# A two-layer transformer block on one core: expert rows added to their tokens in DRAM instead of stored by slot and gathered

## The chip, the core and the metric

The kernel runs on one core of one Trainium2 chip. The metric is the device time of one execution in microseconds; the time before is the median of three runs. The engines are PE (TensorE, matrix products), DVE (VectorE), ACT (ScalarE), POOL (GpSimd) and SP (SyncE, which here only issues transfers).

## What is computed

2048 tokens of 512 channels go through two adaLN layers. Layer 0 has windowed attention and a mixture of experts, layer 1 sliding-window attention and a Hadamard-mixed feed-forward part. The part that matters, cut down:

```python
probs = softmax(x @ gate_weight.T)                      # 64 experts
top_val, top_idx = lax.top_k(probs, 8)
top_val = top_val / top_val.sum(-1, keepdims=True)      # routing weight
# the last four choices of a token are sent to the most similar "primary"
# expert where that one is similar enough
rerouted = mapping[top_idx]; rerouted[:, :4] = top_idx[:, :4]
gate, up = split(expert_gate_up(x))                     # 192 + 192 wide
y = expert_down(silu(gate) * up)                        # 512 wide
out = zeros.at[tok].add(y * w)                          # sum over a token's 8 rows
x = x + gate_mlp * out                                  # adaLN residual, before layer 1
```

Everything is float32. A token's eight rows lie in up to eight expert tiles.

## The kernel before, in words

The program is a sequence of six stages with a barrier of all engines after each. Within a stage every engine has its own written-out list of turns, and semaphores join them; the function `schedule` of each stage says which tile each part of a turn works on. Nothing is planned at run time but the number of expert tiles in use.

1. **Setup** (0 to 32 us): constants, the modulation vectors of layer 0.
2. **First attention** (32 to 319 us), 16 tiles of 128 tokens. Its turn ends with the router: for each pair of tiles `choose` (L659 to L691) takes the eight best experts, writes a one-hot `route_hot` (token, choice, expert) in bfloat16 and the weights `route_w`. SP also fills the expert output `y_moe` in DRAM past its first 64 tiles (L418, L419: 32 transfers of 1 MB) and stores the normalized tokens `h_moe` (L424).
3. **Routing** (319 to 383 us). The rows of all experts are laid out in slots of tiles of 128, each expert rounded up to whole tiles, at most 192 tiles (`SLOTS`), here 158. PE counts and ranks (L899 to L932), DVE works out where each expert's tiles begin, and L943 to L949 build `slot_rows`, the token of each slot, as products of one-hot matrices paced by ACT and DVE. `map_row` (L940, L1041) holds where each expert was moved.
4. **Experts** (383 to 1212 us), one turn for each slot tile `g`. `turn(before, g, after)` has `before = g - 1` and `after = g + 1`. PE transposes the hidden rows of `before` (L1157), multiplies tile `g` by the gate and up weights (L1166), transposes the input rows of `after` (L1175) and multiplies `before` by the down weights (L1183). POOL gathers the 128 token rows of `after` by an indirect transfer (L1136 to L1146), after PE has transposed the tile two before. DVE makes the hidden rows (L1282) and scales the output rows into `y` (L1287). ACT stores `y` (L1214) into `y_moe` at its slot. SP loads 1.15 MB of weights for each of 64 experts into a ring of four. The loop is unrolled by two; iterations beyond the tiles in use are skipped by a test on each engine. In the first 15 double turns DVE also runs `place` (where each token's eight rows lie: `pos_u`) and `finish_mod`, in the next 15 a transform of the feed-forward weights.
5. **Second attention** (1212 to 1748 us), 16 tiles. Before a tile's statistics POOL gathers its eight expert rows from `y_moe` (L1440 to L1447; eight indirect transfers of 256 KB a tile, spread over the turn) and DVE adds them into `x_res` with their weights (L1719 to L1723, eight additions). Then come the statistics (L1725 to L1734), the reciprocal root on POOL (L1457), the normalization that opens the next turn on DVE (L1742), modulation on POOL (L1459, L1461), and PE's transposes (L1578) and products (L1599 for q, L1608 for k and v). In a turn, g is the tile gathered, y the tile added, p the tile projected, f, s, a and w the later steps.
6. **Feed-forward** (1748 us to the end), PE near its peak in float32r.

The lines around which the change turns:

```python
                        nc.gpsimd.indirect_dma_start(out=xg[:, b], out_offset=None, in_=h_moe,
                                                     in_offset=bass.IndirectOffsetOnAxis(ap=st_tok[:, b], axis=0)).then_inc(x_in[b], 16)
...
                        act.dma_start(dst, y[:, b]).then_inc(y_stored[b], 16)
```

## Time and profile before

| | |
|---|---|
| median of 3 runs | 2322.02 us (2320.09 to 2323.6) |
| the profiled execution's own time | 2322.45 us |
| its span, first to last instruction | 2320.6 us |
| PE busy | 2024.3 us (87%) |
| DVE busy | 1095.3 us (47%) |
| ACT busy | 742.9 us (32%) |
| POOL busy | 725.6 us (31%) |
| transfers, mean rate | 302.32 MB, 130 GB/s |
| DMA_INDIRECT L1145 (expert inputs) | 160, mean 990 ns of POOL |
| DMA_INDIRECT L1446 (expert outputs) | 128, mean 966 ns of POOL |

A busy time is the time in which an instruction of the engine ran. Where a row says `[1.54 <-PE bank L1183]`, the engine stood idle for 1.54 us before that instruction and was released by PE's line 1183. Issuing an indirect transfer is work of POOL; "to landing" is from the start of the issue to the arrival of the data. PEclk is the granted clock as a share of the full one. The times of the stages above are read from where their first instructions start.

### The profile page before, as it was taken

Reading aid. Unit: us, or ns where it says so; the run is one execution under the profiler, and the core shown is the slowest. Engines: PE = TensorE matmul, PEld = TensorE weight load, DVE = VectorE, ACT = ScalarE, POOL = GpSimd, SP = SyncE. Lnnn points to the kernel's source line nnn. Section 1 sums busy time; section 2 is a strip of 40 time slices with the busy share of each in tenths; the row PEclk is TensorE's granted clock in tenths of the full one; section 3 lists DMA queues with packets and bytes.
Section 4 is the critical chain, followed back from the end, with each engine's and each line's share of the span. In section 5 each row is a group of like instructions: output and inputs, shape, how many; then the busy total and the mean of one; then the engine's idle time right before and its main releaser. Section 6 shows DMA issues by size and latency. Waiting matters only on the chain. (4 is left out here: it accounts for less than half of the span.)

```text
span 2320.6 us, 38481 instructions
## 1 busy us (share of the span) xinstructions
PE 2024.3 (87%) x11149; PEld 1332.4 (57%) x11150; DVE 1095.3 (47%) x2952; ACT 742.9 (32%) x1743; POOL 725.6 (31%) x1163
## 2 busy tenths in 40 slices
PE   4799867999999999999971588888866999999998
PEld 2667534555555555555531255555545878878787
DVE  2467667555553222222114577777634444443432
ACT  0233226222222222222210255555642333222322
POOL 0243311222333333333226677777402101011000
PEclk7799879999999999999985689999987999999999
DMA  6556632565555656656625222223011112121210
GB/s 239 177 211 219 235 116 65 182 214 180 190 182 196 193 191 211 215 195 199 213 94 147 82 82 76 83 79 85 5 43 40 64 55 82 64 81 63 73 64 28
DMA packets 122554, 302.32 MB, mean 130 GB/s; under 512 B 24912, under 2 KB 28624, under 8 KB 122320
## 3 DMA queue, kind: packets, MB, share of 16 engines
q1 hardware_dynamic: 73424, 179.04, 22.7%
q0 software_dynamic: 23040, 75.52, 11.4%
q10 hardware_dynamic: 25984, 46.38, 5.3%
q8 instruction: 63, 1.03, 0.2%
q14 instruction: 43, 0.35, 0.0%
HBM read 216.47 MB, written 83.36 MB: 129 GB/s over the span
## 5 line engine op out<-in xcount | busy, mean ns | idle before, releaser
L1166 PE MATMUL bank<-arena 128*128 x1272 | 445.5, 493 | 10.3 <-issue 9.2
L1166 PEld LDWEIGHTS bank<-arena 128*128 128x128 f32 x1272 | 229.6, 190 | 147.7 <-issue 16.9
L1183 PE MATMUL bank<-arena 96*128 x632 | 297.5, 593 | 0.0
L1287 DVE TENSOR_TENSOR arena<-bank,mod 128x512 f32<-128x512 f32 x158 | 109.3, 692 | 214.8 <-PE bank L1183 214.8
L1904 PE MATMUL bank<-x_hi,w_hi 128*128 128x512 f32 x512 | 200.8, 392 | 6.0 <-DVE x_lo L2037 6.0
L1904 PE MATMUL bank<-x_hi,w_lo 128*128 128x512 f32 x512 | 199.4, 389 | 0.0
L1904 PE MATMUL bank<-x_lo,w_hi 128*128 128x512 f32 x512 | 199.2, 389 | 0.0
L1282 DVE TENSOR_TENSOR arena<-arena,bank 128x192 f32<-128x192 f32 x159 | 56.3, 354 | 301.0 <-ACT arena L1204 300.6
L1199 ACT COPY arena<-bank 96x256 f32<-96x256 f32 x158 | 58.2, 368 | 423.8 <-issue 221.7
L1145 POOL DMA_INDIRECT arena<-h_moe,arena x160 | 158.4, 990 | 75.1 <-issue 74.2
L1144 POOL TENSOR_TENSOR arena<-neg_half 128x1 f32<-128x1 f32 x160 | 31.3, 196 | 461.9 <-PE bank L1175 461.7
L2117 DVE SCALAR_TENSOR_TENSOR ffn_arena<-bank,ffn_arena,mod 128x512 f32<-128x512 f32 x64 | 48.1, 751 | 221.5 <-PE bank L1904 174.7
L1183 PEld LDWEIGHTS bank<-arena 96*128 96x128 f32 x632 | 107.3, 190 | 76.2 <-issue 76.2
L1494 ACT ACTIVATE arena<-arena 128x256 f32<-128x256 f32 x256 | 127.0, 500 | 44.9 <-DVE arena L1701 44.6
L1446 POOL DMA_INDIRECT route_hot<-y_moe,pos_u x128 | 123.7, 966 | 32.1 <-issue 27.7
L1723 DVE SCALAR_TENSOR_TENSOR x_res<-route_hot,route_w,x_res 128x512 f32<-128x512 f32 x128 | 112.8, 881 | 26.6 <-DMA route_hot<-y_moe,pos_u 18.0
L1578 PE MATMUL bank<-ident,down_scale 128*128 128x128 f32 x64 | 14.6, 369 | 124.0 <-POOL down_scale L1461 124.0
L1885 POOL TENSOR_TENSOR ffn_arena<-ffn_arena,neg_half 128x1 f32<-128x1 f32 x16 | 8.8, 548 | 362.0 <-DVE ffn_arena L2051 362.0
L1175 PEld LDWEIGHTS bank<-ident,arena 128*128 128x128 f32 x640 | 80.2, 141 | 58.8 <-issue 28.8
L1904 PEld LDWEIGHTS bank<-x_hi,w_hi 128*128 128x128 f32 x512 | 96.1, 188 | 28.7 <-issue 4.8
L1904 PEld LDWEIGHTS bank<-x_hi,w_lo 128*128 128x128 f32 x512 | 96.1, 188 | 20.3
L1904 PEld LDWEIGHTS bank<-x_lo,w_hi 128*128 128x128 f32 x512 | 96.2, 188 | 19.5
(326 smaller groups left out, 3738.6 us busy)
## 6 DMA issues: line engine op xcount, KB each, us to landing
arena<-in_moe_up SPq DMA_DIRECT2D x64, 768.0 KB, 5.0
y_moe<-arena ACTq DMA_DIRECT2D x158, 256.0 KB, 3.1
y_moe<-mod SPq DMA_DIRECT2D x32, 1024.0 KB
ffn_arena<-in_ffn_up SPq DMA_DIRECT2D x64, 512.0 KB, 3.2
arena<-in_moe_down SPq DMA_DIRECT2D x64, 384.0 KB, 5.8
arena<-in_L_wmod SPq DMA_DIRECT2D x12, 1024.0 KB, 11.3
x_res<-in_L_attn_x SPq DMA_DIRECT2D x1, 4096.0 KB, 18.5
h_moe<-arena SPq DMA_DIRECT2D x16, 256.0 KB, 6.8
```

Of the source, the lines that this page charges most:

```text
L1145: nc.gpsimd.indirect_dma_start(out=xg[:, b], out_offset=None, in_=h_moe, in_offset=bass.IndirectOffsetOnAxis(ap=st_tok[:, b], axis=0)).the ...
L1166: mm = nc.tensor.matmul(psum[2 + b][:, 0:2 * FI], xgT[:, b, k], up_ring[:, bass.ds((e % RING) * UPW + k * 2 * FI, 2 * FI)], start=(k == 0) ...
L1175: mm = nc.tensor.transpose(psum[b][:, k * P:(k + 1) * P], xg[:, b, k * P:(k + 1) * P], ident[:])
L1183: mm = nc.tensor.matmul(psum[6 + b][:], hiddenT[:, b, n], down_ring[:, bass.ds((e % RING) * DOWNW + n * C, C)], start=(n == 0), stop=(n == 1))
L1199: nc.scalar.copy(hiddenT[:, b], psum[4 + b][0:FH, 0:2 * P].rearrange("p (n q) -> p n q", n=2)).then_inc(hT_out, 1)
L1282: nc.vector.tensor_tensor(hidden[:, b], gate_act[:, b], psum[2 + b][:, FI:2 * FI], ALU.mult).then_inc(hidden_done, 1)
L1287: nc.vector.tensor_tensor(y[:, b], psum[6 + b][:], mod[:, 0, 5], ALU.mult).then_inc(y_out, 1)
L1446: nc.gpsimd.indirect_dma_start(out=yg[:, j], out_offset=None, in_=y_moe, in_offset=bass.IndirectOffsetOnAxis(ap=pos_u[:, t, j:j + 1], axis ...
L1494: nc.scalar.activation(some, some, ACT.Exp, bias=nmx[:, t % 2, n:n + 1], scale=-1.0, accum_out=esum[:, t % 2, n:n + 1]).then_inc(exp_done, 1)
L1723: nc.vector.scalar_tensor_tensor(x_res[:, t], yg[:, j], route_w[:, t, j:j + 1], x_res[:, t], ALU.mult, ALU.add).then_inc(y_sum, 1)
L1904: mm = nc.tensor.matmul(bank, x, y, start=(n == 0), stop=(n == len(passes) - 1))
L2117: nc.vector.scalar_tensor_tensor(inner, up_bank[:], scales[:, 1, f:f + 1], gate_act[:, b], ALU.mult, ALU.mult).then_inc(inner_done, 1)
```

## The change

`y_moe`, its fills and its gathers go. Two arrays `x_sum[0]` and `x_sum[1]` in DRAM take the token rows: in the first attention SP stores the residual `x_res` into the first and zeros into the second. In the expert stage tile t's output rows are added to `x_sum[t % 2]` by an indirect transfer that POOL issues with an add (`compute_op=ALU.add`), one row per slot, to the row of its token; unused slots go to 128 spare rows. It waits for the y of that tile and is issued one turn late, behind the gather. Before y's buffer is written again, the add of the tile two before must have landed. The routing weight is multiplied into the hidden rows on DVE: the weight of a token for each expert is made in the first attention and in the routing stage (eight more transposes and 16 more products on PE, four more copies on ACT) and stored behind the token's row in `h_moe`, so that the gather brings 576 numbers instead of 512. DVE reads the expert of the tile into a register and copies the column. `place`, `map_row`, `pos_u`, `route_hot` and `route_w` go. In the second attention SP loads a tile from both arrays two turns ahead, DVE adds the two once, and the statistics and the reciprocal root move forward in the turn.

```diff
-        h_moe = dram("h_moe", [S, C])
-        y_moe = dram("y_moe", [SLOTS * P, C])
+        h_moe = dram("h_moe", [S + P, C + E])
+        x_sum = [dram(f"x_sum{b}", [S + P, C]) for b in range(2)]
...
@@ first attention, choose(pair) @@
-                    st.did(nc.vector.tensor_tensor(route_w[:, 2 * pair:2 * pair + 2], top[:], over(l2[:, 4], TOPK), ALU.mult))
+                    st.did(nc.vector.tensor_tensor(two, two, over(l2[:, 4], E), ALU.mult))
+                    st.settle()
+                    for half, dense in enumerate((routed.first, routed.second)):
+                        st.did(nc.vector.tensor_tensor(dense[:, pair].rearrange("p (t e) -> p t e", e=E), two, routed.multi[:, pair, half], ALU.mult))
...
@@ first attention, SP @@
-                        for g in (E + 2 * s * FILL, E + (2 * s + 1) * FILL):
-                            sp.dma_start(y_moe[g * P:(g + FILL) * P].rearrange("(g p) c -> p g c", p=P), some).then_inc(filled, 16)
+                        sp.dma_start(x_sum[1][s * P:(s + 1) * P], zero[:, 0:C]).then_inc(filled, 16)
...
+                        sp.dma_start(x_sum[0][z * P:(z + 1) * P], x_res[:, z]).then_inc(x_kept, 16)
...
@@ routing: SP, ACT, PE, DVE @@
+                sp.wait_ge(w_out, 2)
+                sp.dma_start(h_moe[0:S, C:].rearrange("(t p) e -> p t e", p=P), routed.second.rearrange("p i (t e) -> p (i t) e", e=E)).then_inc(w_stored, 16)
...
+                for n in range(2):
+                    act.wait_ge(wT_mm, n + 1)
+                    nc.scalar.copy(routed.secondT[:, 4 * n:4 * n + 4].rearrange("p i n -> p (i n)"), psum[2 + n][:]).then_inc(wT_out, 1)
...
+                pe.wait_ge(moves_wide, 1)
+                for n in range(2):
+                    for i in range(4):
+                        at = psum[6 + n][:, i * P:(i + 1) * P]
+                        nc.tensor.matmul(at, routed.secondT[:, 4 * n + i], moves_f, start=True, stop=False)
+                        mm = nc.tensor.matmul(at, ident[:], routed.first[:, 4 * n + i], start=False, stop=True)
+                    mm.then_inc(w_mm, 1)
...
-                st.did(nc.vector.tensor_copy(slot_rows[:, 0:SLOTS], psum[1][:, 0:SLOTS]))
+                step(ts(empty, psum[1][:, 0:SLOTS], 0.0, pad_row, ALU.is_equal, ALU.mult))
+                st.did(nc.vector.scalar_tensor_tensor(slot_rows[:, 0:SLOTS], psum[1][:, 0:SLOTS], -1.0, empty, ALU.add, ALU.add))
...
@@ experts, POOL @@
+                def add_rows(t, b):
+
+                    wait_tile(pool, y_out, 1, t)
+                    st.did(nc.gpsimd.tensor_copy(st_dst[:, b], column(t)))
+                    st.settle()
+                    st.did(nc.gpsimd.tensor_tensor(spare, neg_half[:], neg_half[:], ALU.add))
+                    nc.gpsimd.indirect_dma_start(out=x_sum[b], out_offset=bass.IndirectOffsetOnAxis(ap=st_dst[:, b], axis=0), in_=y[:, b],
+                                                 in_offset=None, compute_op=ALU.add).then_inc(y_added[b], 16)
...
                     if after is not None:
                         t, b, half = after
                         wait_tile(pool, x_in[b], 16, shift(half, -1))
+                        wait_tile(pool, w_read, 1, shift(t, -2))
...
+                    if before is not None:
+                        t, b, half = before
+                        if not isinstance(t, int) or t:
+                            add_rows(shift(t, -1), 1 - b)
+                used = schedule(pool, turn, st, POOL_M)
+                pairs = (used + 1) // 2
+                st.base, st.k = pairs * POOL_M + (st.first - 2 * POOL_M), 0
+                add_rows(pairs * 2 + -1, 1)
+                for b in range(2):
+                    pool.wait_ge(y_added[b], pairs * 16)
...
@@ experts, ACT: the store of y goes @@
-                        act.dma_start(dst, y[:, b]).then_inc(y_stored[b], 16)
...
@@ experts, DVE @@
-                        nc.vector.tensor_tensor(hidden[:, b], gate_act[:, b], psum[2 + b][:, FI:2 * FI], ALU.mult).then_inc(hidden_done, 1)
+                        wait_tile(dve, w_read, 1, t)
+                        nc.vector.scalar_tensor_tensor(hidden[:, b], gate_act[:, b], row_w[:, b:b + 1], psum[2 + b][:, FI:2 * FI],
+                                                       ALU.mult, ALU.mult).then_inc(hidden_done, 1)
...
-                        wait_tile(dve, y_stored[b], 16, shift(half, -1))
+                        wait_tile(dve, y_added[b], 16, shift(half, -1))
                         nc.vector.tensor_tensor(y[:, b], psum[6 + b][:], mod[:, 0, 5], ALU.mult).then_inc(y_out, 1)
+                    if after is not None:
+                        t, b, half = after
+                        e = dve.value_load(tile_expert[0:1, bass.ds(t, 1)], min_val=0, max_val=E - 1)
+                        wait_tile(dve, x_in[b], 16, half)
+                        wait_tile(dve, hidden_done, 1, shift(t, -2))
+                        nc.vector.tensor_copy(row_w[:, b:b + 1], xg[:, b, bass.ds(e + C, 1)]).then_inc(w_read, 1)
...
@@ second attention, SP @@
+                def rows_in(t):
+
+                    if t >= XB:
+                        sp.wait_ge(x_sums, t - XB + 1)
+                    sp.dma_start(x_res[:, t], x_sum[0][t * P:(t + 1) * P]).then_inc(x_in[t % XB], 16)
+                    sp.dma_start(xb[:, t % XB], x_sum[1][t * P:(t + 1) * P]).then_inc(x_in[t % XB], 16)
...
@@ second attention, POOL: gather() and its calls go; the reciprocal root moves to the turn's end @@
-                gather(0, range(0, TOPK))
...
+                    if y is not None:
+                        pool.wait_ge(stats, y + 1)
+                        if y:
+                            pool.wait_ge(xhat, y)
+                        nc.gpsimd.tensor_tensor(r1[:, 1:2], st1[:, 7:8], neg_half[:], ALU.pow).then_inc(rstd, 1)
...
@@ second attention, DVE: eight add_expert() a tile go @@
+                def join_rows(t):
+                    dve.wait_ge(x_in[t % XB], 32 * (t // XB + 1))
+                    nc.vector.tensor_tensor(x_res[:, t], x_res[:, t], xb[:, t % XB], ALU.add).then_inc(x_sums, 1)
...
                     if a is not None:
                         sums(a)
+                    if y is not None:
+                        join_rows(y)
...
+                    if y is not None:
+                        statistics(y)
                     if s is not None:
                         maxima(s, 2)
```

## Rows read from the trace of the kernel before

**Rows 1.** Two stages (start:end): us, busy PE, PEld, DVE, ACT, POOL; clock, DMA, GB/s
```profile
383.00:1212.00 829.00, 800.94 (x2860) 451.20 (x2860) 289.67 (x749) 204.62 (x477) 252.33 (x640) 0.99 0.57 187
1212.00:1748.00 536.00, 379.03 (x2530) 231.83 (x2530) 343.86 (x975) 246.32 (x753) 323.42 (x375) 0.84 0.26 77
```

**Rows 2.** timeline of one expert tile: start us, us, engine line op
```profile
903.27 0.60 PE L1175 MATMUL bank<-ident,arena 128*128 128x128 f32 x4
...
903.71 1.88 PE L1183 MATMUL bank<-arena 96*128 x4
...
904.04 0.19 POOL L1144 TENSOR_TENSOR arena<-neg_half 128x1 f32<-128x1 f32 x1 [2.93 <-PE bank L1175]
...
904.69 0.99 POOL L1145 DMA_INDIRECT arena<-h_moe,arena  x1 [0.47 <-issue]
...
905.68 0.20 POOL L1139 COPY arena<-slot_rows 128x1 int32 x1
905.73 0.69 DVE L1287 TENSOR_TENSOR arena<-bank,mod 128x512 f32<-128x512 f32 x1 [1.54 <-PE bank L1183]
...
905.96 0.19 POOL L1141 TENSOR_TENSOR arena<-neg_half 128x1 f32<-128x1 f32 x1
...
908.24 0.60 PE L1175 MATMUL bank<-ident,arena 128*128 128x128 f32 x4
```

**Rows 3.** instructions of line L1157, whole run
```profile
L1157 PE MATMUL bank<-ident,arena x316: 270/274/314, 397.9 to 1197.0; 128*96 128x128 f32 x158
```

**Rows 4.** timeline of VectorE in the second attention: heads of turns
```profile
1267.68 0.55 DVE L1742 TENSOR_SCALAR down_scale<-x_res,arena 128x512 f32<-128x512 f32 x1 [7.46 <-POOL arena L1457]
...
1298.02 0.55 DVE L1742 TENSOR_SCALAR down_scale<-x_res,arena 128x512 f32<-128x512 f32 x1 [7.44 <-POOL arena L1457]
...
1624.19 0.55 DVE L1742 TENSOR_SCALAR down_scale<-x_res,arena 128x512 f32<-128x512 f32 x1 [1.64 <-POOL arena L1457]
...
1649.15 0.54 DVE L1742 TENSOR_SCALAR down_scale<-x_res,arena 128x512 f32<-128x512 f32 x1
...
1673.25 0.69 DVE L1748 TENSOR_TENSOR mod<-bank,mod 128x512 f32<-128x512 f32 x1 [3.25 <-PE bank L1653]
```

**Rows 5.** busy time in stretches of the second attention (columns as in rows 1)
```profile
1212.00:1240.00 28.00, 0.00 (x0) 0.00 (x0) 7.13 (x15) 0.00 (x0) 16.96 (x21) 0.50 0.88 255
...
1457.00:1511.00 54.00, 45.70 (x318) 28.51 (x314) 41.01 (x117) 30.74 (x94) 39.05 (x46) 0.91 0.28 81
```

**Rows 6.** timeline: single instructions of first attention and routing
```profile
123.40 3.73 PE L554 MATMUL bank<-arena 128*128 128x128 f32 x32
...
232.41 0.35 DVE L749 TENSOR_SCALAR arena<-bank,arena 128x128 f32<-128x128 f32 x1 [2.31 <-PE bank L563]
...
319.78 1.07 ACT L841 CAST arena<-bank 128x512 bf16<-128x512 f32 x2 [8.21 <-PE bank L906]
```

**Rows 7.** instructions of line L1161: PE's register load
```profile
L1161 PEldq TENSOR_LOAD <-tile_expert x159: 296/303/841, 390.5 to 1195.8; - x159
```

**Rows 8.** instructions of line L1145: whole run, then landing within 900 to 950 us
```profile
L1145 POOL DMA_INDIRECT arena<-h_moe,arena x160: 986/986/1353, 386.2 to 1191.1; - x160
...
DMA to landing us min/median/max: 3.3/3.8/4.4
```

**Rows 9.** timeline of VectorE: end of the expert stage
```profile
1212.01 0.10 DVE L1313 MEMSET arena<- 128x1 f32 x2 [9.23 <-issue]
```

**Rows 10.** timeline of PE: first q product of the second attention
```profile
1246.59 5.06 PE L1599 MATMUL bank<-arena,mod 128*128 128x512 f32 x8 [0.77 <-ACT mod L1514]
```

**Rows 11.** DMA queues within 900 to 1000 us: packets, MB, share of 16 engines
```profile
q1 hardware_dynamic: 2304, 10.62, 31.7%
q0 software_dynamic: 1600, 5.24, 18.3%
q10 hardware_dynamic: 2880, 5.24, 14.1%
```

More of the change, by code:

```diff
@@ L907, in _ @@
                     mm.then_inc(secT_mm, 1)
+                for n in range(2):
+                    for i in range(4):
+                        mm = nc.tensor.transpose(psum[2 + n][:, i * P:(i + 1) * P], routed.second[:, 4 * n + i], ident[:])
+                    mm.then_inc(wT_mm, 1)
                 for f in range(HAD0):
@@ L1372, in schedule @@
                 tile = lambda t: t if 0 <= t < NT else None
[L1373 to L1374 removed]
+                for m in range(-3, NT + 2):
+                    turn(y=tile(m + 3), p=tile(m + 2), f=tile(m + 1), s=tile(m), a=tile(m - 1), w=tile(m - 2))
             def slot(t, c):
@@ L1787, in turn @@
                         nc.vector.tensor_tensor(x_res[:, w], ba[:], x_res[:, w], ALU.add).then_inc(x_out, 1)
-                    if y is not None:
-                        for j in range(5, TOPK):
-                            add_expert(y, j)
-                    if y is not None:
-                        statistics(y)
                     if s is not None:
```

179 lines of the change are left out of this document (74 added, 105 removed).

## The prediction

> **What bounds the kernel now.** I read three views in this order: the busy time by stage, the timeline of a tile or turn inside a stage, and the durations of single instructions. The chain of waits ends in the last stage (the feed-forward of layer 1), which the change leaves alone, so it says nothing here. The stage table [rows 1] shows the two stages that matter: the experts take 829.0 us with PE busy 800.9, the attention after them 536.0 us with PE busy only 379.0. The expert stage is PE's, the second attention is a chain across engines.
>
> Inside an expert tile [rows 2] PE goes from one product to the next without a gap; the transposes L1175 recur after 908.24 - 903.27 = 4.97 us. POOL has slack: it waits for the transposes, starts its gather at 904.69, and idles again. Over the stage the 158 pairs of L1157 run from 397.9 to 1197.0 [rows 3], so a tile takes 799.1 / 157 = 5.09 us on average; the 0.12 above 4.97 (19 us in all) falls mostly into the part where VectorE also does side work. In the attention, L1742 opens a turn of VectorE [rows 4]. From tile 2 (1298.02) to tile 14 (1624.19) there are 12 turns of 27.18 us. Two of them hold 45.70 us of PE work, the first 28 us of the stage none at all [rows 5].
>
> **The change part by part.**
>
> *First attention.* The choosing of experts for a pair of tiles gets three 128-wide products and a settle for one 16-wide product. The 128-wide L749 takes 0.35 us [rows 6], overlapped a little less: +0.8 us on VectorE. Seven of eight times it is covered, as VectorE then waits 2.31 us for PE before L749. The last is exposed: +0.8. SP's 32 fills of 1 MB become 19 of 256 KB or little more and 16 stores of 256 KB; nothing waited for the fills, so 0.
>
> *Routing.* ACT gets two copies ahead of the work PE waits for; two such took 1.07 us (L841) [rows 6]. PE gets 16 products of 128x128 in float32; 32 took 3.73 us (L554), so 1.9, and a release, 0.2. The table's end becomes two dependent operations instead of one, +0.4. The table's own 40 us are paced by ACT and only shift. SP's store of the weights stands ahead of three weight loads; they shift too. Sum +3.6.
>
> *Expert stage, what goes.* The plain stores leave ACT's queue, and 16 placings leave VectorE. VectorE waits for PE before L1287 [rows 2], so this gives at most the 19 us above.
>
> *Expert stage, what comes.* VectorE reads a register and copies one column per tile; PE's register load takes 0.30 us [rows 7], so with its arithmetic and the copy 0.7 us, done before POOL needs it (below). The decisive part is POOL's order. In turn g it gathers tile g+1 and then adds tile g-2, whose rows are ready only one turn later. So the gather of k+4 stands behind the add of k; PE's turn k+3 transposes k+4 before it multiplies out k+2. This closes a loop from y(k) ready to y(k+2) ready. Its length from [rows 2]: release 0.1; index copy to addition 0.28, to transfer 0.65: 0.93; the add's issue *a*; two small operations and the same lead for the gather, 0.28 + 0.28 + 0.65 = 1.21; the landing *L* from the gather's start; release 0.1; transposes to y ready, 906.42 - 903.27 = 3.15. Together 5.49 + a + L, for two tiles. The issue of a gather lasts 0.99, at most 1.35 us; its landing is 3.8 in the median and 4.4 at most in 50 us of this stage [rows 8]. Accumulating transfers are not in this trace. Nearest is the gather itself, so I take values just above its own: a = 1.10, L = 4.0 (its rows also grow from 2048 to 2304 bytes). The loop is 10.59, a tile 5.30 us: 157 x 5.30 = 832.1 against 799.1, **+33.0**. Bounds: with 0.99 and 3.8 a tile takes 5.14 (+8); with 1.35 and 4.4 it takes 5.62 (+83). Below nothing: if the loop is shorter than 9.94, PE keeps its 4.97, -19. VectorE's column is ready about 0.9 after y(k), POOL asks for it about 2.1 after: covered. If that cover is gone, half of the excess is added per tile. The reuse of the y buffer leaves the add 2 x 4.97 - 0.69 (L1287) - 1.0 (its lead) = 8.2 us to land, against 3.8 for a gather: covered.
>
> *End of the expert stage.* VectorE's last 9.23 us are empty passes of the loop [rows 9]. POOL makes the same passes and then adds the last tile. It starts them when the add of the tile before is issued, some 3.1 us before VectorE starts its own (5.3 for the tile, less 0.1 + 0.93 + 1.10), so it is through at 6.1 where VectorE was at 9.2. Then come 0.93 and the add's landing: 4.0 gives +1.8, twice that +5.8. I take +3.5, nearer to the gather's.
>
> *Start of the second attention.* The first q product starts at 1246.59 [rows 10]. Before it come eight gathers one after another. Without them it waits for the weights. The first 28 us move 255 GB/s [rows 5], 7.1 MB, of which 16 gathers are 4.2 MB; three tiles of the new loads are 1.6 MB. 4.5 MB at that rate are 17.6 us, so with the spread of the issues 1232.5: -14.1. Tiles 1 and 2 then wait 7.46 and 7.44 us for the reciprocal root on POOL, which stands behind gathers [rows 4]; that goes: -14.9. Sum **-29.0**.
>
> *Turns.* The turn that starts at 1624.19 has the adds but no gathers: 24.96 us. The next has neither: L1748, about 0.5 after the head of a turn, comes at 1673.25, so 1672.75 - 1649.15 = 23.6 [rows 4]. The new turn keeps a 0.7 us join and the statistics, which mostly fall into waits for PE. I take 23.8: 12 x (27.18 - 23.8) + 1.2 = **-41.8**. What is late next is PE: its 22.9 us of work a turn [rows 5].
>
> **Sum.** 0.8 + 3.6 + 33.0 + 3.5 - 29.0 - 41.8 = -29.9 against the profiled execution, 2322.45 (span 2320.6 and 1.85 around it): 2292.5. That execution is 0.4 above the median of the three runs, 2322.02, so I say 2292.
>
> **A rule against the change.** The 20 gathers in 100 us occupy queue 0 for 18.3% of 16 engines, 0.92 us each; with the stores and the weights the engines are 64% busy [rows 11]. No row shows an add. The Trainium skill, "Collectives: The Full Stack", section "The bandwidth ceiling: the fold count and why AG ≠ RS ≠ AR", says that a reducing transfer sends two source reads down one read ring and so halves the rate. By that rule the add would occupy the engines about twice as long as a copy; the first rival below gives that time.
>
> **The rivals.** *Slower: the gather is late behind the add.* Place: the software queue in the expert stage. Price: each us more in a + L costs 157 / 2 = 78.5 us; from 0.38 us above my value (29.9 / 78.5) the change loses. If an add occupies the queue 0.92 us longer than a gather and the next gather meets all of that, L is 3.8 + 0.92 = 4.7, and with a = 1.35 the loop is 11.54: 5.77 a tile, +107 instead of +33: **2366**. For it: the engines are busy in bursts already, and the loop has no slack. Against: the gather starts 2.3 us after the add, which may be gone by then. *Faster: the loop stays hidden.* PE keeps 4.97, -19 instead of +33: **2240**. Against: that needs a + L of 4.45, below the median gather of 4.8. *Turns shrink less.* If join and statistics land on the path, turns stay at 24.96, 15 us less gain: **2307**. Against: VectorE is idle for 3.25 us before L1748 at the end of the turn from 1649.15 [rows 4], so it has room.
>
> **How the numbers follow.** Forecast 0.42, late gather 0.36, hidden loop 0.12, longer turns 0.10. The forecast's own range is 2267 to 2342, from the bounds of a and L. The range for 8 in 10, 2257 to 2390, leaves out most of the hidden loop and a late gather beyond 5.92 us a tile. A change under 0.2% (4.6 us) is about what this measurement can't tell from none. Faster by more than that: 0.36 of the forecast, the hidden loop 0.12, 0.07 of the longer turns, 0.55. Within: 0.03 + 0.03 + 0.02 = 0.08. Slower: 0.03 of the forecast and 0.34 of the late gather, 0.37.
>
> **What would show it.** Right: L1157 pairs every 5.3 us, each L1175 released by the gather, with POOL starting it some 2.2 us after the add; L1742 every 23.8 us; the first q product 19 us after the stage's start. Wrong: an issue of the add well over 1.1 us, landings of the gather over 4.5, VectorE's register read or the free y buffer in the loop instead; or PE without waits at 4.97.

## The result, and the profile after

The changed kernel takes 2445.21 us (median of 4 runs, 2431.36 to 2450.8) against 2321.06 (4 runs beside it): ratio 1.0525, 95% interval 1.0479 to 1.0571. It is slower, and the forecast of 2292 us, its range (to 2390) and its likeliest sign were wrong. The profiled execution took 2443.06 us, its span 120.7 us more than the one of before. Where only one execution of an experiment's kernel was timed, the text compares it with this profiled one.

The page of the changed kernel: span, PE's share, the clock in 40 slices, and four of the costliest groups (busy us, mean ns, idle time ahead and what ended it).

```profile
span 2441.3 us, 39558 instructions
...
PE 2092.7 (86%) x11188; PEld 1332.8 (55%) x11189; DVE 990.6 (41%) x2920; ACT 742.0 (30%) x1747; POOL 896.2 (37%) x1464
...
PEclk7899888999999999999999967999997999999999
...
L1219 PE MATMUL bank<-arena 128*128 x1272 | 460.3, 506 | 22.2 <-issue 18.7
...
L1174 POOL DMA_INDIRECT x_sum<-arena x158 | 251.3, 1590 | 52.4 <-issue 51.9
L1325 DVE TENSOR_TENSOR arena<-bank,mod 128x512 f32<-128x512 f32 x158 | 109.4, 692 | 378.7 <-PE bank L1236 378.7
...
L1228 PE MATMUL bank<-ident,arena 128*128 128x128 f32 x640 | 100.7, 280 | 82.1 <-DMA arena<-h_moe,arena 81.8
```

L1228, the transposes of a gathered tile, waited 81.8 us on the matmul side and 122.3 us on the weight-load side for the gather's DMA; L1175 of [rows 2], its counterpart, ran without a gap. VectorE's L1325 idles 378.7 us for PE. The add (L1174) holds POOL 1590 ns each time. The hidden transposes, the counterpart of L1157 in [rows 3], show the pace:

```profile
L1210 PE MATMUL bank<-ident,arena x316: 270/274/421, 406.0 to 1405.5; 128*96 128x128 f32 x158
```

From 406.0 to 1405.5 are 999.5 us for 157 tiles, **6.37 us a tile** against 5.09. The busy time in four stretches (columns as in [rows 1]): the expert stage, its even middle, the second attention, and nine of its turns:

```profile
400.00:1411.00 1011.00, 887.17 (x2856) 461.99 (x2855) 279.31 (x789) 204.00 (x476) 562.88 (x1100) 0.97 0.66 157
500.00:1150.00 650.00, 565.07 (x1812) 293.20 (x1810) 199.29 (x557) 129.71 (x303) 360.77 (x703) 0.96 0.67 159
1426.00:1846.00 420.00, 346.84 (x2514) 211.48 (x2514) 230.60 (x837) 241.70 (x750) 169.02 (x193) 0.92 0.11 31
1548.00:1749.00 201.00, 188.29 (x1432) 115.81 (x1431) 129.05 (x469) 136.10 (x424) 93.59 (x108) 1.00 0.07 23
```

PE's share fell to 87% in the middle of the expert stage, and rose to 94% in the turns. The kernel before, in the middle of its expert stage:

```profile
500.00:1150.00 650.00, 645.86 (x2317) 364.63 (x2316) 217.04 (x519) 165.35 (x387) 201.06 (x514) 1.00 0.60 197
```

So PE's granted clock fell too, from 1.00 to 0.96: it has two levels, 2.4 and 1.2 GHz, and a mean of 0.96 over 650 us is some 50 us at the lower one. One such stretch in the changed kernel (PE's timeline, then the stretch in the columns of [rows 1]):

```profile
1127.49 1.12 PE L1228 MATMUL bank<-ident,arena 128*128 128x128 f32 x4 [3.72 <-DMA arena<-h_moe,arena]
1128.44 3.77 PE L1236 MATMUL bank<-arena 96*128 x4
```

```profile
1126.10:1132.90 6.80, 5.41 (x11) 2.83 (x12) 0.65 (x1) 0.81 (x2) 0.00 (x0) 0.50 0.36 95
```

PE had waited 3.72 us for a gather, the clock stood at 0.50, and the four products into y took 3.77 us instead of 1.88. As an estimate, 50 us at half the clock cost PE at most 25 us of these 650, or 0.25 us a tile. The heads of turns in the second attention, which answer to [rows 4] (L1773 is L1742 of before, L1779 is L1748):

```profile
1483.76 0.55 DVE L1773 TENSOR_SCALAR down_scale<-x_res,arena 128x512 f32<-128x512 f32 x1 [3.29 <-POOL arena L1513]
...
1749.40 0.54 DVE L1773 TENSOR_SCALAR down_scale<-x_res,arena 128x512 f32<-128x512 f32 x1
...
1845.60 0.69 DVE L1779 TENSOR_TENSOR mod<-bank,mod 128x512 f32<-128x512 f32 x1 [5.36 <-PE bank L1686]
```

And the seam between the stages: POOL's last adds, the first load of the next stage, and the first q product (L1632), which answers to [rows 9] and [rows 10]:

```profile
1407.31 1.61 POOL L1174 DMA_INDIRECT x_sum<-arena  x1 [0.33 <-issue]
1415.46 0.18 POOL L1171 COPY arena<-slot_rows 128x1 int32 x1 [6.55 <-issue]
...
1416.27 1.57 POOL L1174 DMA_INDIRECT x_sum<-arena  x1 [0.35 <-issue]
...
1426.60 0.34 SPq L1438 DMA_DIRECT2D x_res<-x_sum  x1
...
1447.96 6.55 PE L1632 MATMUL bank<-arena,mod 128*128 128x512 f32 x8 [11.09 <-DMA arena<-in_meta_head]
```

The difference, cut at the same places of both traces (head 0 is the first turn's):

```
stretch                                   before    after     change   forecast
start to the first gather                 386.2     392.4      +6.2      +4.4
to the first hidden transposes             11.7      13.6      +1.9       0
157 tiles of experts                      799.1     999.5    +200.4     +33.0
last hidden transposes to the next stage   16.3      21.1      +4.8      +3.5
to the first q product                     33.3      21.4     -11.9     -14.1
to head 2                                  51.4      35.8     -15.6     -14.9
head 2 to head 14                         326.2     265.6     -60.5     -40.6
to the last L1748, L1779                  101.0      96.2      -4.8      -1.2
the rest                                  595.4     595.7      +0.3       0
```

The attention gave 92.8 us, 22 more than forecast. The experts took 200.4 us, 167 more than forecast. That second number is the error.

### The profile page after: what moved, and what is told of

Same layout as the page of the kernel before. It is cut to its first block and busy times, and to the rows that moved or that the text cites. A ratio compares the mean times of both kernels' runs of the same rounds, so it can differ in the third digit from the quotient of the medians.

```text
span 2441.3 us, 39558 instructions
## 1 busy us (share of the span) xinstructions
PE 2092.7 (86%) x11188; PEld 1332.8 (55%) x11189; DVE 990.6 (41%) x2920; ACT 742.0 (30%) x1747; POOL 896.2 (37%) x1464
## 3 DMA queue, kind: packets, MB, share of 16 engines
q1 hardware_dynamic: 68240, 163.61, 20.4%
q8 instruction: 63, 1.03, 0.2%
## 5 line engine op out<-in xcount | busy, mean ns | idle before, releaser
L1219 PE MATMUL bank<-arena 128*128 x1272 | 460.3, 506 | 22.2 <-issue 18.7
L1236 PE MATMUL bank<-arena 96*128 x632 | 325.9, 640 | 28.9 <-issue 27.7
L1219 PEld LDWEIGHTS bank<-arena 128*128 128x128 f32 x1272 | 236.1, 196 | 183.3 <-issue 60.7
L1174 POOL DMA_INDIRECT x_sum<-arena x158 | 251.3, 1590 | 52.4 <-issue 51.9
L1325 DVE TENSOR_TENSOR arena<-bank,mod 128x512 f32<-128x512 f32 x158 | 109.4, 692 | 378.7 <-PE bank L1236 378.7
L1319 DVE SCALAR_TENSOR_TENSOR arena<-arena,bank 128x192 f32<-128x192 f32 x159 | 66.0, 415 | 301.4 <-ACT arena L1255 301.4
L1255 ACT ACTIVATE arena<-bank 128x192 f32<-128x192 f32 x159 | 52.7, 331 | 415.7 <-PE bank L1219 415.7
L1228 PE MATMUL bank<-ident,arena 128*128 128x128 f32 x640 | 100.7, 280 | 82.1 <-DMA arena<-h_moe,arena 81.8
L1228 PEld LDWEIGHTS bank<-ident,arena 128*128 128x128 f32 x640 | 76.1, 142 | 150.3 <-DMA arena<-h_moe,arena 122.3
L1183 POOL COPY arena<-slot_rows 128x1 int32 (+1 forms) x160 | 115.7, 723 | 92.4 <-issue 84.1
L1171 POOL COPY arena<-slot_rows 128x1 int32 (+1 forms) x158 | 28.6, 181 | 307.8 <-DVE arena L1325 301.3
L1260 ACT COPY arena<-bank 128x512 f32<-128x512 f32 x160 | 93.8, 586 | 112.5 <-PE bank L1228 101.8
```

What stands on the lines that cost most here:

```text
L1174: nc.gpsimd.indirect_dma_start(out=x_sum[b], out_offset=bass.IndirectOffsetOnAxis(ap=st_dst[:, b], axis=0), in_=y[:, b], in_offset=None, c ...
L1183: st.did(nc.gpsimd.tensor_copy(st_tok[:, b], column(t)))
L1219: mm = nc.tensor.matmul(psum[2 + b][:, 0:2 * FI], xgT[:, b, k], up_ring[:, bass.ds((e % RING) * UPW + k * 2 * FI, 2 * FI)], start=(k == 0) ...
L1228: mm = nc.tensor.transpose(psum[b][:, k * P:(k + 1) * P], xg[:, b, k * P:(k + 1) * P], ident[:])
L1236: mm = nc.tensor.matmul(psum[6 + b][:], hiddenT[:, b, n], down_ring[:, bass.ds((e % RING) * DOWNW + n * C, C)], start=(n == 0), stop=(n == 1))
L1260: nc.scalar.copy(xgT[:, b].rearrange("p k n -> p (k n)"), psum[b][:]).then_inc(xT_out, 1)
```

## The experiments

The theory is the forecast's own mechanism at another size: a loop from y(k) to y(k+2), over the add of k, the gather of k+4 behind it, its landing and PE. The rivals were traffic alone, VectorE's register read, and the free y buffer. One turn of the loop in the changed kernel, from the timeline (start us, duration us, engine and line; L1143 is the load of an expert's weights):

```profile
904.40 0.69 DVE L1325 TENSOR_TENSOR arena<-bank,mod 128x512 f32<-128x512 f32 x1 [1.95 <-PE bank L1236]
...
905.27 0.18 POOL L1171 COPY arena<-slot_rows 128x1 int32 x1 [0.58 <-DVE arena L1325]
...
906.05 1.59 POOL L1174 DMA_INDIRECT x_sum<-arena  x1 [0.33 <-issue]
...
908.67 1.01 POOL L1189 DMA_INDIRECT arena<-h_moe,arena  x1 [0.28 <-issue]
...
913.51 0.60 PE L1228 MATMUL bank<-ident,arena 128*128 128x128 f32 x4
...
913.95 1.88 PE L1236 MATMUL bank<-arena 96*128 x4
...
915.97 0.69 DVE L1325 TENSOR_TENSOR arena<-bank,mod 128x512 f32<-128x512 f32 x1 [1.48 <-PE bank L1236]
916.02 0.35 SPq L1143 DMA_DIRECT2D arena<-in_moe_up  x1
...
921.97 0.33 PE L1228 MATMUL bank<-ident,arena 128*128 128x128 f32 x1 [2.70 <-DMA arena<-h_moe,arena]
```

y(k) ends at 905.09. The add starts 0.96 later, the gather 2.62 after the add, its transposes at 913.51, 4.84 after the gather; y(k+2) (L1325 of 915.97) ends at 916.66. Of these 4.84 the gather took 3.79: it had landed at 912.46, and PE was still at its product for the tile between (L1219, until 913.67 in the timeline). The next gather, at 914.91, has the weights issued at 916.02 behind it, lands 7.01 us after its start, and PE, which waits 2.70 us for it, starts its transposes at 921.97: 7.06 us. The means in the table below are taken over all such loops between 500 and 1150 us of each trace (98 to 117 of them): from the end of each L1325 the next add, the next gather, the transposes that it releases, and the end of the y behind them. "Tile" is the 157 tiles' stretch divided, as above.

```
us, mean           y to add   add to gather   gather to PE   PE to y   loop    tile   time
forecast             1.03         2.31            4.10         3.15    10.59   5.30   2292
changed kernel       0.98         2.65            5.72         3.61    12.97   6.37   2443
index copies ahead   0.64         2.02            5.89         3.53    12.08   6.02   2389
early reads on PE    0.99         2.65            5.65         3.32    12.62   6.18   2410
half columns         0.99         2.65            4.62         3.53    11.78   5.85   2363
scatter, no add      0.99         2.16            4.77         3.42    11.34   5.64   2329
no weight loads      0.99         2.65            4.26         3.41    11.31   5.66   2328
pause, no transfer   0.59         2.49            4.58         3.24    10.90   5.42   2296
no transfer                                                                    5.14   2246
```

**No transfer.** The add's transfer and VectorE's wait for it go:

```diff
-    nc.gpsimd.indirect_dma_start(out=x_sum[b], ..., in_=y[:, b], in_offset=None, compute_op=ALU.add).then_inc(y_added[b], 16)
-    wait_tile(dve, y_added[b], 16, shift(half, -1))
```

> The expert stage without the add's transfer and without VectorE's wait for it: the expert rows are left out of x_sum. POOL still copies the index and waits for y before it gathers. Loop theory: 3.58 us from y to gather less the 1.59 us of the issue, landing 3.8, 3.6 us to the next y: 9.4 us for two tiles, under PE's 9.94; so PE bound, 5.0 to 5.15 us a tile, 2443 - 157 x 1.22 to 1.37 = 2228 to 2251 us. VectorE theory (register read and column copy keep PE waiting): still above 5.3 us a tile, above 2275 us.

Measured: 2245.53 us, 5.14 us a tile (L1206 from 401.0 to 1207.6). The whole loss of the expert stage hangs on the transfer. VectorE's read and column copy, still there, cost 0.05 us a tile at most.

**Pause.** The same with POOL held in its place:

```diff
+    st.did(nc.gpsimd.memset(route[:, 0:1650], 0.0))
```

> As the kernel without the add's transfer, but POOL fills 1650 unused columns in its place, about 1.5 us: POOL is held as long as by the add's issue, and no DMA engine is. The expert rows are left out again. Loop theory: 2.0 + 1.5 + 3.8 + 3.6 = 10.9 us for two tiles, 5.45 a tile, 2443 - 157 x 0.92 = 2299 us; so of the 1.25 us a tile that the changed kernel loses, about 0.3 to 0.4 are the time of the issue and the rest the transfers' (longer landings and queueing). Traffic theory alone: no difference to the kernel without a transfer, 5.0 to 5.15 us a tile.

Measured: 2296.43 us, 3 us from the theory's number; 5.42 us a tile. The fill (group of the kernel with the pause):

```profile
L1174 POOL MEMSET route<- x119: 1468/1472/1477, 503.0 to 1146.6; 128x1650 f32 x119
```

Of the 1.23 us a tile between no transfer and the changed kernel, holding POOL for 1.47 us explains 0.28. That is less than the issue of an add is worth, as the pause isn't quite in its place: from y to the gather are 3.08 us here (0.59 and 2.49) and 3.63 in the changed kernel (0.98 and 2.65). With these 0.55 added to its loop of 10.90 a tile would be at 5.72 (an estimate), so holding POOL explains at most 0.58 of the 1.23. So traffic alone falls as a theory, and the issue alone isn't enough.

**Scatter.** The transfer writes rows over instead of adding them:

```diff
-    in_offset=None, compute_op=ALU.add).then_inc(y_added[b], 16)
+    in_offset=None).then_inc(y_added[b], 16)
```

> The same indirect transfer on POOL, in the same place, without the addition: rows of y are written over the rows of x_sum, not added to them (so the output lacks the sums). It tells what the accumulation costs beyond a scatter. If the addition doubles what a transfer occupies in the queue and lengthens the issue, the issue falls from 1.59 to about 1.0 us and the gather lands about 0.9 us earlier: loop 1.5 us shorter, a tile 5.6 us, about 2325 us. If the 1.59 us belong to every transfer that goes from the chip's memory to scattered rows of DRAM, only the landing gets shorter: a tile 5.9 to 6.0 us, about 2375 us. If traffic alone mattered, bytes written are the same and bytes read are fewer: between the two.

Measured: 2328.87 us, 5.64 us a tile, as the first case of the expectation had it. The scatter's issue, and the software queue within 500 to 1150 us (packets, MB, share of 16 engines), in the kernel with the scatter:

```profile
L1174 POOL DMA_INDIRECT x_sum<-arena x115: 1005/1013/1488, 500.3 to 1146.4; - x115
```

```profile
q0 software_dynamic: 18313, 63.76, 30.1%
```

The same queue in the kernel without the transfer, with its gathers alone:

```profile
q0 software_dynamic: 10128, 37.31, 20.4%
...
arena<-h_moe,arena POOLq DMA_INDIRECT x126, 3.6
```

And the changed kernel, its issues and landings, then its queues, in the same window:

```profile
L1174 POOL DMA_INDIRECT x_sum<-arena x100: 1587/1592/1605, 503.9 to 1145.7; - x100
...
DMA to landing us min/median/max: 4.7/5.0/8.4
...
L1189 POOL DMA_INDIRECT arena<-h_moe,arena x101: 1012/1017/1027, 500.6 to 1148.3; - x101
...
DMA to landing us min/median/max: 3.6/4.5/7.5
```

```profile
q0 software_dynamic: 22497, 55.91, 44.4%
q1 hardware_dynamic: 10369, 47.59, 22.6%
```

The issue is 1.01 us for a scatter and 1.59 for an add. For the occupation: 20.4% of 650 us over 126 gathers is 1.052 us each. The changed kernel has 44.4%, 288.6 us, less 101 gathers at 1.052, 106.3 us: 182.3 us for 100 adds, **1.82 us each**. The scatter kernel has 30.1%, 195.7 us, less 115 gathers: 74.7 us for 115, 0.65 each. These are estimates: they put all that changes beside an add down to the add. The same working gives 2.08 us in the kernel without weight loads (55.8%, 116 adds, 115 gathers). By them an add occupies the engines 2.8 times as long as a scatter of the same rows, and 1.98 times the 0.92 us of a gather of before [rows 11]. The Trainium skill, "Collectives: The Full Stack", section "The bandwidth ceiling: the fold count and why AG ≠ RS ≠ AR", has, for collectives, the reducing transfer at half the rate of the copying one. The trace agrees with that by the gather's 0.92; against a scatter the measured price is higher.

**Half the columns.** Adds of 256 columns into tables of 256:

```diff
-    nc.gpsimd.indirect_dma_start(out=x_sum[b], ..., in_=y[:, b],
+    nc.gpsimd.indirect_dma_start(out=x_half[b], ..., in_=y[:, b, 0:C // 2],
```

> The changed kernel with adds of 256 instead of 512 columns, into tables of 256 columns (half of each expert row is left out). Rows, instructions and the place of the add stay. If what an add occupies goes by bytes, its 1.8 us on the engines fall to about 0.9, and the gather behind it lands 0.5 to 0.9 us sooner: a tile about 6.0 us, 2365 to 2400 us. If it goes by rows: no change in either, 2430 to 2450 us. The issue on POOL should stay at 1.59 us if it goes by rows, and fall towards 1.0 us if by bytes.

Measured: 2363.43 us, 2 us below the expected range, 5.85 us a tile. Issue and queue in that kernel, in the same window:

```profile
L1175 POOL DMA_INDIRECT x_half<-arena x111: 1587/1592/1605, 499.3 to 1146.4; - x111
```

```profile
q0 software_dynamic: 24805, 47.05, 36.0%
```

36.0% of 650 us less 111 gathers leaves 117.2 us for 111 adds, 1.06 each: the occupation goes mostly by bytes. The issue did not move, 1.59 us: it goes by rows and by the addition. The gather reaches PE 1.1 us sooner, more than expected.

**No weight loads.**

```diff
-    sp.dma_start(up_ring[...], one(up)...).then_inc(w_in[r], 16)
-    sp.dma_start(down_ring[...], one(down)...).then_inc(w_in[r], 16)
+    sp.sem_inc(w_in[r], 32)
```

> The changed kernel without the expert weights' transfers inside the stage (48 and more loads of 1.15 MB left out; products use the weights that lie there). It tells whose traffic makes the gather late. If the weights' bursts do, the longest landings (7.5 us against a median of 4.5) go and with them most of PE's waits: two tiles fall by 1 us or more, a tile to 5.8 us or less, 2355 us or less. If it is the add ahead of it in POOL's own queue, the median landing stays above 4.0 us and a tile at 6.1 us or more: 2400 us or more.

Measured: 2328.09 us, 5.66 us a tile; gather to PE 4.26 us instead of 5.72. The first case, though the gather still takes longer to reach PE than the 4.1 us of the forecast. The weights' bursts make 0.71 us of a tile (6.37 less 5.66), but only beside the adds: with the weights and without the add a tile is 5.14. The add without the weights makes the other 0.52 (5.66 less 5.14), if a kernel with neither, which wasn't run, takes 5.14 too.

**Index copies ahead.** Both index copies of a turn are made before POOL waits for y (shortened):

```diff
+    prepare_add(*old)                      # y_added wait, copy into st_dst
+    st.did(nc.gpsimd.tensor_copy(st_tok[:, b], column(t)))
+    st.settle()
+    add_rows(old[0], old[1])               # waits for y, one small operation, the add
     ...
     nc.gpsimd.indirect_dma_start(out=xg[:, b], ...)
```

> The changed kernel with both index copies of a turn made before POOL waits for y, the order of its two transfers unchanged. In the changed kernel's timeline 0.96 us lie between the end of y and the add, 1.03 us between the end of the add's issue and the gather; a release, one small operation and the transfer's own lead, 0.55 each, stay. So the two-tile loop is 0.9 us shorter. Loop theory: 157 / 2 x 0.9 = 70 us less than 2443, about 2373 us. Traffic theory, or any in which the loop isn't what sets the pace: no change, 2430 to 2450 us.

Measured: 2388.67 us. The two stretches lost 0.34 and 0.63 us, 0.97 together as the expectation's working had it (0.9). A tile fell by 0.35 where half of 0.9 would be 0.45, so the time is 16 us above the expected 2373: the gather reaches PE later again, 5.89 us instead of 5.72. That the shorter loop meets the weights more often is a guess. The loop sets the pace.

**Column copy ahead of y.** On the changed kernel, in VectorE's turn:

```diff
+    if after is not None: ... nc.vector.tensor_copy(row_w[:, b:b + 1], xg[:, b, bass.ds(e + C, 1)]).then_inc(w_read, 1)
     if before is not None: ... nc.vector.tensor_tensor(y[:, b], ...).then_inc(y_out, 1)
-    if after is not None: ... nc.vector.tensor_copy(row_w[:, b:b + 1], ...).then_inc(w_read, 1)
```

> The changed kernel with VectorE's register read and column copy placed ahead of the y evacuation of the same turn instead of behind it, POOL unchanged. Loop theory: the column is ready before POOL asks for it in either order, and y of k is no earlier: within 15 us of 2443. Register-read theory (it sits between y and the gather): a column earlier by 0.6 to 1.0 us in the loop, 50 to 80 us less.

Measured: 2458.04 us, 15 us more than the changed kernel's profiled run, at the edge of the expectation, and 7 us above its slowest: no gain. The register read on VectorE is not in the loop.

**Early reads on PE.** Both reads of an expert number at the head of PE's turn:

```diff
     def turn(before, g, after):
+        if g is not None:
+            e = pe.value_load(tile_expert[0:1, bass.ds(g[0], 1)], ...)
+        if before is not None:
+            e_down = pe.value_load(tile_expert[0:1, bass.ds(before[0], 1)], ...)
```

> The changed kernel with both of PE's reads of an expert number made at the head of the turn, nothing else moved. In the changed kernel the read for the product into y (L1232, 0.30 us and arithmetic) stands behind the wait for the gather, so where PE waits there it lies in the two-tile loop; the timeline has 0.3 to 0.4 us more from the transposes to y than the kernel before. Loop theory: 0.3 to 0.5 us off each loop, 157 / 2 x 0.3 to 0.5 = 24 to 39 us less than 2443: 2404 to 2419 us. If the reads are covered: within 10 us of 2443.

Measured: 2409.58 us, within the expected 2404 to 2419; PE to y fell from 3.61 to 3.32 us. The read is hidden only as long as PE doesn't wait; behind the wait for the gather it lies in the loop.

**The later add.** POOL adds tile g-3 instead of g-2, still behind the gather of g+1:

```diff
-    if not isinstance(t, int) or t:
-        add_rows(shift(t, -1), 1 - b)
+    if not isinstance(t, int) or t > 1:
+        add_rows(shift(t, -2), b)
```

> POOL adds tile g-3 instead of g-2 in turn g, still after the gather of tile g+1; so the gather of k+4 no longer stands behind the add of k, but behind the add of k-1, whose rows have been ready for a turn. Nothing else is moved: the same transfers, bytes and instructions. Loop theory (the stage is paced by: y of tile k ready, add issued, gather of k+4 issued and landed, its transposes, y of k+2): the loop is gone, a tile falls from 6.37 us to between 5.0 and 5.3 us, so 157 x 1.07 to 1.37 = 168 to 215 us less than the changed kernel's 2443, 2228 to 2275 us, below the kernel before. Rival, traffic (the adds load the DMA engines so that gathers and weights come late whatever the order): a tile stays above 6.0 us and the time above 2385 us. Rival, VectorE's register read and column copy, or the wait for the free y buffer: unchanged or, for the y buffer, worse, since the add is issued no earlier: above 2430 us.

Measured over 3 rounds: 2342.35 us (2339.96 to 2346.67), ratio to before 1.009, interval 1.0059 to 1.0122; 5.74 us a tile. That is 103 us better, so the loop is the main cause, but 67 us above the expected range, and not its 5.0 to 5.3 us a tile. What took its place, from VectorE's waits between 500 and 1150 us in this kernel (us in total, times, longest), and from its timeline (L1175 is the add, L1190 the gather, L1334 the column copy, L1184 POOL's index copy):

```profile
DVE arena L1328 <- DMA x_sum<-arena: 120.4, 33, 6.1
```

```profile
902.78 1.59 POOL L1175 DMA_INDIRECT x_sum<-arena  x1
...
903.51 0.35 SPq L1143 DMA_DIRECT2D arena<-in_moe_up  x1
...
910.78 0.69 DVE L1328 TENSOR_TENSOR arena<-bank,mod 128x512 f32<-128x512 f32 x1 [3.75 <-DMA x_sum<-arena]
...
911.82 0.15 DVE L1334 COPY arena<-arena 128x1 f32 x1 [0.35 <-issue]
...
912.14 0.18 POOL L1184 COPY arena<-slot_rows 128x1 int32 x1 [3.26 <-DVE arena L1334]
...
913.15 1.01 POOL L1190 DMA_INDIRECT arena<-h_moe,arena  x1 [0.28 <-issue]
```

The add of 902.78, issued just ahead of the weights, landed 8 us later, and y (L1328) waited 3.75 us for its buffer. Behind y stood the column copy, behind it POOL's index copy, and the next gather started only at 913.15. The forecast had priced this buffer as covered, with 8.2 us to land. With the add issued a good deal after y, and a burst of weights on it, the cover was gone.

**Later add, column first.** The later add together with the VectorE order of "column copy ahead of y" (its diff stands there):

> The kernel with the later add (2342 us, 5.74 us a tile), and the column copy ahead of the y evacuation. In that kernel's timeline y waits up to 3.9 us for the add of two tiles before to land, VectorE's column copy stands behind this y, and POOL's next gather behind the column copy. If that is the loop which took the place of the first, cutting it brings a tile to 5.3 to 5.5 us, 2275 to 2305 us; the wait of y for the landed add stays. If the landing of gathers in a busy queue is what sets the pace: no more than 15 us less, 2327 to 2342 us.

Measured: 2315.3 us (10 runs, 2306.68 to 2327.47), ratio 0.9982, interval 0.9965 to 0.9999; 5.58 us a tile. 27 us less, so the chain behind y was real, but 10 us short of the expected range.

**With the index copies ahead.** On top of that, in POOL's turn (shortened):

```diff
+    wait_tile(pool, y_added[b], 16, shift(half, -2))                 # the add that last used st_dst[b]
+    st.did(nc.gpsimd.tensor_copy(st_dst[:, b], column(t - 2)))       # for the add of g-3
     st.did(nc.gpsimd.tensor_copy(st_tok[:, b], column(t)))           # for the gather of g+1
     st.settle()
+    wait_tile(pool, w_read, 1, shift(t, -2))
     wait_tile(pool, xT_mm, 1, shift(t, -2))
     nc.gpsimd.indirect_dma_start(out=xg[:, b], ...)
     wait_tile(pool, y_out, 1, t)
-    st.did(nc.gpsimd.tensor_copy(st_dst[:, b], column(t)))
     nc.gpsimd.indirect_dma_start(out=x_sum[b], ..., compute_op=ALU.add)
```

> The same, with the two index copies made before POOL waits for the transposes and for y, so that both transfers start some 0.5 us earlier after what releases them. The add must have landed before y of two tiles on; from the add's issue to its landing 8 us were seen where weights come in between. Earlier issue takes 0.5 to 1 us from that wait where it shows: 5.2 to 5.4 us a tile, 5 to 20 us less than the kernel without it, 2260 to 2295 us.

Measured: 2288.5 us (4 runs), ratio 0.9854, interval 0.9833 to 0.9875; 5.42 us a tile. That is 27 us less, where 5 to 20 were expected. PE hardly waits for gathers there (1.7 us between 500 and 1150 us). It idles 29.7 us ahead of its gate product (L1223) instead, 22.8 of them in that window. PE's register read ahead of that product (ns min/median/max), in this kernel and then in the one with the pause:

```profile
L1218 PEldq TENSOR_LOAD <-tile_expert x159: 299/628/1129, 398.4 to 1255.5; - x159
```

```profile
L1211 PEldq TENSOR_LOAD <-tile_expert x159: 297/303/320, 400.5 to 1258.2; - x159
```

The read ahead of the same product tells more in other traces: 0.33 us in the median and 1.07 at most in the changed kernel, 0.52 and 1.02 without the weight loads, 0.31 and 0.68 with half the columns, 0.31 and 0.84 with a scatter, never over 0.32 without any transfer. So the slow reads need no weight loads, and in these kernels they come with indirect transfers to DRAM, most with adds of full width.

**Early reads, in two steps.** First the read for the gate product and VectorE's, then the one for y too (`e_down`, as in the diff of the early reads):

```diff
     def turn(before, g, after):                                    # PE
+        if g is not None:
+            e = pe.value_load(tile_expert[0:1, bass.ds(g[0], 1)], ...)
     def turn(before, g, after):                                    # VectorE
+        if after is not None:
+            e = dve.value_load(tile_expert[0:1, bass.ds(after[0], 1)], ...)
```

> The best so far (later add, column first, index copies ahead, 2288 us) with the expert number of PE's and VectorE's next product read at the head of the turn. In that kernel's trace PE's read ahead of L1223 takes 0.63 us in the median against 0.30 before the change, up to 1.1, and PE is idle 29 us ahead of L1223. If these reads are what is left, 15 to 30 us less: 2260 to 2275 us. If the reads are slow wherever they stand because of POOL's issue and PE waits just as long elsewhere: within 5 us of 2288.

Measured: 2254.56 us (4 runs), ratio 0.9722, interval 0.9683 to 0.9761; 5.19 us a tile. 34 us less, somewhat more than expected.

> The best version so far (2254.6 us, 5.19 us a tile) with PE's other read, the one for the product into y, at the head of the turn too. PE is idle only 7.6 us ahead of that product in 650 us there, so at most some 10 us less: 2244 to 2256 us. If two reads at the head cost more than they give (the transposes of hidden behind them start late): 2255 to 2270 us.

Measured: 2251.6 us (2250.42 to 2253.29), ratio 0.9701, interval 0.9679 to 0.9723. The intervals of the two overlap, so the last step isn't told from nothing. The profile's page and the hidden transposes of this last kernel:

```profile
span 2251.5 us, 39244 instructions
...
PE 2007.6 (89%) x11188; PEld 1316.0 (58%) x11189; DVE 972.1 (43%) x2920; ACT 742.6 (33%) x1747; POOL 864.1 (38%) x1304
...
L1218 PE MATMUL bank<-ident,arena x316: 270/274/314, 405.7 to 1216.2; 128*96 128x128 f32 x158
```

810.5 us for 157 tiles is 5.16 us, against 5.09 before the change and 6.37 in it. Its gathers land no sooner: 5.4 us in the median and 8.7 at most between 500 and 1150 us, later than in the changed kernel (4.5 and 7.5). What the new order took away is PE's waiting for them.

## Why the prediction was wrong, point by point

*The expert loop (mechanism right, size wrong).* The forecast put the loop where it is, and held that each us more in a + L costs 78.5 us. It said +33.0 by 10.59 us a loop; the traces show 12.97 in the middle of the stage, and +200.4 over it. Of the loop's 2.38 us too little:

- *L, "values just above its own" = 4.0 us (4.1 with the release):* 5.72 from the gather's start to PE. This is 1.62 of the 2.38 and the step that failed. It has two halves. The landing is one: over the 101 gathers between 500 and 1150 us it is 4.78 in the mean (median 4.5, at most 7.5), 0.78 above the 4.0. The value was taken from gathers of before, which meet no add, and from 50 us of them, where 4.4 was the latest. The same line of before over a wider window:

```profile
DMA to landing us min/median/max: 3.2/3.6/7.4
```

That is from 500 to 1150 us, mean 3.84. Late landings were there already, but 6 of 128 took over 5 us, and in the changed kernel 37 of 101 do. The other half lies behind the landing: from there to PE's transposes are 0.89 in the mean, where the forecast had a release of 0.1. It let PE wait for every gather; in the changed kernel 55 of the 101 landed over 0.3 us before PE came, which was still at the gate product (L1219) that stands ahead of the transposes in its list. The kernel with the pause, without an add, has the same 0.87 there, with landings of 3.70. The runs split the whole: adds of half the bytes bring the 5.72 to 4.62, no weights to 4.26. No step of the forecast had the weights' bursts and the adds together.

- *a = 1.10 us:* 1.59, above the bound of 1.35, which was the slowest gather and no bound for another kind of transfer. The stretch from add to gather grew by only 0.34, as the forecast's 1.21 behind the issue were 1.03 to 1.06 in the changed kernel.
- *PE, 3.15 us from transposes to y:* 3.61. 0.29 of the 0.46 are PE's register read, which came out from under its cover, as the early reads show. Another 0.14 goes with the clock: the 69 of 98 loops in which it stayed at its upper level have 3.47 there (and 5.09 from gather to PE, 12.18 in all); the 29 that touch the lower level have 3.96, 7.22 and 14.84. The forecast had no term for the clock. How much of these long loops it makes itself, and how much the late gather ahead of it, wasn't tried.
- *y to add, 1.03:* 0.98.

*The rival "late gather behind the add"* named this place and the price, and had L = 4.7, a loop of 11.54 and 2366 us. It too had only the adds' own occupation (0.92 us more; measured 1.82 for an add against 0.92 for a gather of before, so 0.90) and not the weights. It deserved more than 0.36: the row for it, engines 64% busy in bursts, stood in the text. With 5.92 us a tile as the far end, the range ended 55 us below the result.

*VectorE's column, "covered":* right, by the kernel without the transfer and by the moved copy. *The free y buffer, "covered":* right in the changed kernel, whose VectorE waits for PE there; it became the next wait once the first loop was cut. More than two y buffers weren't tried.

*Routing and the start, +4.4:* +6.2, and 1.9 more until the pipeline ran. *End of the stage, +3.5:* +4.8. POOL's last pair of adds is 1407.31 and 1416.27; the last waits behind 6.55 us of POOL's own loop passes, then issues for 1.57 us and lands.

*Start of the second attention, -14.1 and -14.9:* -11.9 and -15.6, right. The q product is held by a weight load for 11.09 us, as forecast.

*Turns, 23.8 us:* 265.64 / 12 = 22.14, so -60.5 instead of -40.6. The forecast's floor was 22.9 us of PE work a turn, read at a granted clock of 0.91 [rows 5]. In nine turns of the changed kernel PE worked 188.29 us, 20.9 a turn with the same 159 matmuls, at a clock of 1.00, the upper level of 2.4 GHz, where it had been busy 85% of a turn before and was 94% now. Why the clock rose wasn't tried by itself.

## What to carry to other kernels

A transfer that adds is not one more copy: price its issue and its occupation apart, and take the landing of what stands behind it together with the largest burst that shares the engines. When a loop over two engines and a queue has no slack, it pays the mean landing, not the median, and read that from the whole stage, not from 50 us. What the engine at its end does ahead of the awaited step belongs to the loop too. Before giving up such a change, look at the order: here the add one turn later in POOL's queue, the column copy ahead of y, index copies and register reads ahead of the waits turned 5% slower into 3% faster, with the same work.

## What the runs showed of the hardware that was not expected

- POOL holds its queue 1.59 us for an indirect transfer of 128 rows that adds, against 1.01 for one that writes and 1.02 for one that gathers; half the columns leave it at 1.59.
- An add of 256 KB occupies 16 engines some 1.8 us (2.1 without weight loads), a scatter of the same rows 0.65, an add of half the columns 1.06. These are estimates from the queue's share less its gathers'.
- PE's register load, 0.30 us, took 0.63 us in the median and up to 1.13 in the kernel with later adds, and never over 0.32 in the kernel with the pause, which has the gathers but no adds (in the kernel before, 0.84 at most [rows 7]). It is as slow without the weight loads, up to 1.02. Reads at the head of the turn were back at 0.30 in the median. Why a transfer to DRAM slows it stays open.
- A stage in which PE idles less ran its own products faster: 22.9 us of PE work a turn became 20.9, with a granted clock of 1.00 instead of 0.91. The expert stage shows the reverse: waits of 3 us and more for a gather, such as the 3.72 us of 1127.49, have stretches at half the clock beside them, and there the products into y took 3.77 us instead of 1.88.
